# A first batch's query store ahead of its key reload, and the next key projection ahead of the first scores, in a one-core attention and expert kernel

## The reference, cut to what matters

```
def attention(queries, keys, values):        # queries = layernorm(x), keys = values = ctx_1024
    q = (queries @ Wq + bq), k = (keys @ Wk + bk), v = (values @ Wv + bv), cut into 16 heads
    attn = softmax(q k^T / sqrt(16)); return (attn v) @ Wo + bo
def moe(x):
    gate = softmax over the two largest of x @ Wr + br
    return sum over these two experts of gate * (relu(x @ W1 + b1) @ W2 + b2)
x = x + tanh(g_xattn[0]) * attention(layernorm(x), ctx_1024)
x = x + tanh(g_ffn[0]) * moe(layernorm(x))
```

## Time and profile before

| | us |
|---|---|
| median of 3 runs | 920.37 (916.33 to 920.69) |
| the profiled execution's own time | 913.82 |
| its span, first to last instruction | 912.0 |
| TensorE busy | 775.5 (85% of the span) |
| VectorE busy | 631.8 (69%) |
| ScalarE busy | 415.5 (46%) |
| GpSimd busy | 450.1 (49%) |

### The profile page before, as it was taken

One profiled execution on the slowest core, in us unless ns is written; L12 is line 12 of the kernel. 1 busy time (PEld: TensorE's weight loads), 2 busy tenths in 40 slices (PEclk: granted clock), 3 DMA queues, 4 the chain that ended last, 5 costly groups with the idle time before them and its releaser, 6 DMA issues.

```text
span 912.0 us, 22725 instructions
## 1 busy us (share of the span) xinstructions
PE 775.5 (85%) x6728; PEld 523.9 (57%) x6729; DVE 631.8 (69%) x1270; ACT 415.5 (46%) x784; POOL 450.1 (49%) x453
## 2 busy tenths in 40 slices
PE   4479988888889888754698769999999999999993
PEld 2235555444545555323576457777777777777771
DVE  5568899989997999861557346666666666666663
ACT  2066777766767676661333213333333333333330
POOL 5113334646555554354555625555544455555532
PEclk9699999999999999985899889999999999999998
DMA  4435565566666666542213223323332222232322
GB/s 130 118 106 157 166 198 165 143 165 167 173 173 173 173 173 165 143 130 46 82 28 45 38 24 47 48 45 48 50 50 48 46 46 46 46 52 43 50 34 29
DMA packets 98524, 86.87 MB, mean 95 GB/s; under 512 B 22822, under 2 KB 87532, under 8 KB 98348
## 3 DMA queue, kind: packets, MB, share of 16 engines
q1 hardware_dynamic: 81164, 65.73, 25.8%
q0 software_dynamic: 17024, 20.53, 14.6%
q10 hardware_dynamic: 288, 0.00, 0.0%
HBM read 54.53 MB, written 31.54 MB: 94 GB/s over the span
## 4 chain that ended last, share of the span: by engine, by line
PE 41%; DMA 18%; DVE 16%; issue 13%; POOL 6%; ACT 3%; SPq 2%; POOLq 1%; DVEq 0%; ACTq 0%
PE banks L1680 12%; DMA out_dram<-yb,dest_idx 12%; DVE negmax L1053 5%; PE banks L1666 4%; PE banks L1668 4%; PE banks L1667 4%; PE banks L1583 3%; PE banks L1502 3%; DMA xg<-xn_rows,gather_idx 2%; PE banks L1479 2%; PE banks L1571 2%; DVE stats L977 2%; ACT probs L855 1%; POOL token_lists L650 1%; DMA xres<-in_x 1%
## 5 line engine op out<-in xcount | busy, mean ns | idle before, releaser
L926 ACT ACTIVATE hid<-banks,b_col 128x256 f32<-128x256 f32 x312 | 130.5, 470 | 244.0 <-PE banks L1668 127.2
L1680 PE MATMUL banks<-wall,hh 128*128 x624 | 225.3, 383 | 1.7 <-DVE yb L1426 1.7
L714 POOL DMA_INDIRECT out_dram<-yb,dest_idx x78 | 133.4, 1711 | 169.2 <-issue 67.2
L1666 PE MATMUL banks<-xh,wall 128*128 128x256 f16 x624 | 173.5, 278 | 7.9 <-DVE xl L1364 5.4
L1053 DVE TENSOR_REDUCE negmax<-banks 128x4 f32<-128x1024 f32 x128 | 155.8, 1217 | 26.6 <-PE banks L1550 25.9
L1668 PE MATMUL banks<-xh,wall 128*128 128x256 f16 x624 | 173.5, 278 | 0.0
L1667 PE MATMUL banks<-xl,wall 128*128 128x256 f16 x624 | 173.4, 278 | 0.0
L855 ACT ACTIVATE probs<-banks 128x1024 f32<-128x1024 f32 x128 | 131.1, 1024 | 79.9 <-PE banks L1571 77.9
L1680 PE MATMUL banks<-wall,hl 128*128 x624 | 158.9, 275 | 0.0
L702 POOL DMA_INDIRECT xg<-xn_rows,gather_idx x78 | 88.5, 1135 | 46.0 <-issue 22.9
L1583 PE MATMUL banks<-probs,vaug 128*32 128x256 f32 x1024 | 83.6, 398 | 27.1 <-ACT probs L855 16.9
(11 more groups left out here) (184 smaller groups left out, 1192.8 us busy)
## 6 DMA issues: line engine op xcount, KB each, us to landing
wst<-in_L_ffn_W SPq DMA_DIRECT2D x30, 512.0 KB, 4.8
k_parts<-kparts SPq DMA_DIRECT2D x48, 128.0 KB
ks<-k_parts SPq DMA_DIRECT2D x64, 96.0 KB, 2.2
q_parts<-qparts SPq DMA_DIRECT2D x48, 128.0 KB, 2.0
qs<-q_parts SPq DMA_DIRECT2D x64, 96.0 KB, 2.2
xin<-in_x SPq DMA_DIRECT2D x16, 256.0 KB, 5.1
cin<-in_ctx SPq DMA_DIRECT2D x16, 256.0 KB, 5.4
xres<-in_x SPq DMA_DIRECT2D x16, 256.0 KB, 4.3
```

Source lines behind the costliest of these rows:

```text
L714: nc.gpsimd.indirect_dma_start(out_rows, bass.IndirectOffsetOnAxis(dest_idx[par][:, s:s + 1], 0), yb[par][:, s, :], None, compute_op=ALU.a ...
L926: ins = nc.scalar.activation(hid[half][:, c % (HC // 2), :], banks[:, b, c % 2 * TS:(c % 2 + 1) * TS], ACT.Relu, bias=b1_col[:, ds(e * HC ...
L1666: nc.tensor.matmul(dst, hi, xh[par][:, m, :], start=(m == 0), stop=False)
L1680: ins = nc.tensor.matmul(dst, h_[:, c, s * P:(s + 1) * P], w_, start=(c == 0 and k == 0), stop=(c == HC - 1 and k == 1))
```

## The change

On SP, the first batch's two stores come first, and its reloads follow in the order keys half 0, queries half 0, keys half 1, queries half 1. On TensorE, in the body of batch 0 alone, the second batch's key projection comes ahead of the first `scores_max`. No instruction is added or removed, and no wait is changed.

```diff
             for name in "kq":
                 store_part(0, 0, name)
-                for h in range(2):
+            for h in range(2):
+                for name in "kq":
                     load_part(0, 0, name, h)
...
                 for u in range(8):
                     if attention:
                         scores(m - 1, 1 - par, u)
+                    first_batch = isinstance(m, int) and m == 0
+                    if u == 0 and first_batch:
+                        k(1, 1, 0)
+                        k(1, 1, 1)
                     if maxima:
                         scores_max(m, par, u)
                     if u == 0:
                         if attention:
                             turn_max(m - 1, 1)
-                        if ahead:
+                        if ahead and not first_batch:
                             k(m + 1, 1 - par, 0)
                             k(m + 1, 1 - par, 1)
```

## The result

The changed kernel takes 913.17 us (median of 22 executions, 908.14 to 924.32), the kernel before, measured beside it, 920.67 us (22 executions, 912.9 to 926.82). One execution of the changed kernel, the one of 924.32 us, counts as slow and is left out of the ratio. The medians lie 7.5 us apart; the ratio, which is not simply that of the medians, is 0.9933, with a 95% interval from 0.9914 to 0.9952: 6.2 us less (4.4 to 7.9), where 5.0 was forecast. The change made the kernel faster, by some 0.7%, which is little more than a measurement can tell.

A forecast was written before the change was run, and what follows sets the result against it. The bound was a relay of key and query stores and reloads through memory before the first score, then the second batch's key projection. Gains of 2.75 and 2.22 us make 4.97: 920.37 - 4.97 = 915.4 us, range 911.5 to 919.3.

The forecast's parts named there:

- The stores: On SP, query stores ahead of the key reloads start at 21.64 us, bringing TensorE's first score 2.75 us earlier, to 27.34.
- The key projection: On TensorE, the second batch's key projection starts near 24.0, takes 1.47 to 2.74 us, wholly within the query reload wait.
- The cover at the dearer price: Slack on TensorE between the moved key projection at the half clock and the first score: 0.6 us.
- The key low half: On VectorE, the second batch's key low half follows the first maximum without its 2.25 us wait, gaining 2.22 us.
- The sum: At VectorE's second maximum, 2.75 us from the stores plus 2.22 from the key projection wait: 4.97 us, carried to the end.
- The clock: TensorE's granted clock keeps its old pattern, half from 26 us; if its changes move, the gain is 3.3 to 6.5 us.
- The upper end: Full TensorE clock from the first score on: total gain about 6.5 us, time 913.9; chance 0.15.
- The cap: The second batch's query reload, from `q_low` on, limits the full clock's further gain to some 0.5 us.
- Rival 3: Query stores collide with key transfers, giving back all the stores' gain; only 2.2 us remain, time 918.2; chance 0.08.
- Rival 4: A transfer or queue in the steady bodies sets the pace and takes the gain back, time 920.4; chance 0.10.
- Rival 5: Early scores leave the clock at half into the second batch, costing 8 to 10 us, time about 925; chance 0.05.
- The profile's span: The whole profiled execution of the changed kernel was to end near 907 us.

The follow-up runs named there:

- changed_again: The changed kernel, unaltered, measured once more beside three other kernels; ratio 0.9961 to the kernel before, median 920.98 us.
- stores_only: Against the changed kernel: the second batch's key projection put back behind the first scores, the new order of stores and reloads kept; ratio 0.9986 to the kernel before.
- projection_twice: Against the changed kernel: the second batch's 12 key projection matmuls done twice, first into a bank nothing reads; ratio 0.9921 to the kernel before, median 917.74 us.
- projection_only: Against the changed kernel: stores and reloads put back in the old order, the key projection kept ahead of the first scores; ratio 0.999 to the kernel before.
- before_again: The kernel before, unaltered, measured against itself; ratio 1.0006.
- filled: Against the changed kernel: matmuls nothing reads added in TensorE's waits of batch 0, 12 and six times 4; ratio 0.9899 to the kernel before, median 915.29 us.
- two_pairs: Against the changed kernel: scores of batch 0 go by turns into two pairs of accumulator banks; ratio 0.9928 to the kernel before.
- filled_two_pairs: Against the changed kernel: both the unread matmuls in batch 0's waits and two pairs of score banks; ratio 0.9877 to the kernel before, 914.23 us.

## Why the prediction was right, point by point

- **The stores.** First score forecast 2.75 us earlier. Counted from the key store it was 2.3 (changed_again), 2.6 (stores_only) and 3.1 us (first profile). The working held: 0.98, 1.96 and 2.24 us of before were 1.07, 1.94 and 2.25. It did put the query's low half on the chain, with the query stores at 21.64 behind it; what it left out is how far that instant varies from execution to execution: the query store was issued 0.04 us behind the end of the key stores' issuing in the first profile and 1.05 us behind it in changed_again. The term was right in its middle and has a spread of 1 us that it did not have before.
- **The key projection.** Forecast at 24.0 for 1.5 to 2.7 us; it was at 23.54 for 1.47. The cover at the dearer price was forecast at 0.6 us; projection_twice used up 2.78 and kept 0.33.
- **The key low half.** Forecast to gain 2.22; projection_only gained 2.28.
- **The sum.** Forecast 4.97; 4.85 in changed_again, 5.65 in the first profile, 0.8 of it the length of the query projection. The last maximum was forecast at 43.4, which is 23.7 behind the first key store; it came at 22.95 and 23.95. The mechanism up to the second maximum is shown by these instants. That the gain goes through to the end is not seen in any pair of profiles, only in the times, and the two measurements of the change give 6.2 and 3.6 us: that the first lies so near the forecast is in part luck.
- **The clock.** I took the pattern of before, with 3.3 and 6.5 us as ends. In the changed kernel the clock does fall, at 28.4 us instead of 25.9, and rises again in places that differ between executions. By the third key projection the changed kernel had gained 5.7 us (31.24 - 25.51) and 4.7 (31.24 - 26.52), within the two ends, while before_again is itself 0.8 us off before. The upper end was too low: filled gained 7.7 us (31.24 - 23.54), 0.5 of it by a first score earlier than forecast. The cap that I had set, the query reload of the second batch, did not hold there: in that kernel the score behind it waited 1.20 us for VectorE and not for a transfer. It did bind in the first profile of the changed kernel, in two_pairs and in filled_two_pairs, whose scores waited 1.47, 1.26 and 1.43 us for that reload.
- **Rival 3, transfers that collide,** is out: the landing of the query stores took 1.94 us. The Trainium skill (DMA: Bandwidth & Descriptors, Latency and other measured facts) gives memory access 2 us under high load; the trace shows no such rise here.
- **Rival 4, a gain taken back,** looked true in the first profile, whose second batch is 5.7 us early and whose end is late, which I had named as a sign of being wrong. It was one execution: the medians keep the gain, the jump behind the ninth batch lies in 8 us at the half clock, and the 6.6 us lost behind the last batch, of which the lower clock from 380 to 400 us may be a part, are not traced further. That an execution's fate in the loop is unaffected by the change is what the medians suggest; it was not tested by itself. **Rival 5** did not come about: the half clock at 45.5 to 48.7 cost 1.1 us on the projection (2.56 against 1.47) and ended there.
- **The profile's span** was forecast near 907 and was 916.6. The step that failed there is the use of two single executions as a pair: executions of one kernel spread over some 10 us, twice the effect.

## What to carry to other kernels

Where one queue serves two trips through memory, issue both stores ahead of the first reload, and interleave the reloads by what the first consumer needs. Put ready work into the wait so gained, and ask afterwards what the old order had been hiding: here the query projection came onto the chain. An effect of 0.5% is read from instants counted from a common event in the traces, and its time from many executions, never from the difference of two profiled spans.

## What the runs showed of the hardware that was not expected

- Matmuls that nothing reads, 12 and six times 4, kept the granted clock at 1.00 from 26 to 44 us, where it was 0.72 without them, and the kernel was 5.7 us faster in the median (915.29 against 920.98). Some 2 us of that are the clock's in the first body; where the rest comes from is open, and projection_twice differs from the same kernel by 3.2 us with all instants of the first body within 0.15 us.
- In the loop TensorE worked for 8 us without a pause at the half clock (224 to 232 us of the first profile), with 54 matmuls; the 8 us of the kernel before that are shown beside it held 93 at the full one.
- Two more reloads of 96 KB ahead of the query reload delayed its landing by 0.3 us beyond the 0.6 us of their issuing: 2.48 us from the last issue to the landing, against 2.12 to 2.25 in the profiles of changed, changed_again and projection_twice.
